# A chunked state-space layer with a mixture of low-rank adapters on one core: who turns x of chunk 1 to tokens in the paired groups

## What is computed

```python
proj = jnp.einsum('bld,pd->blp', hidden_states, in_proj_w)      # gate | x, B, C | dt
xBC = jax.nn.silu(conv)                                          # x: 64 heads of 64; B, C: 8 groups of 128
dt_p = jax.nn.softplus(dt + dt_bias)
dA = jnp.exp(dt_p * A)
dtx = dt_p[..., None] * x
def step(state, inp):
    dA_t, dtx_t, B_t, C_t = inp
    state = state * dA_t[..., None, None] + dtx_t[..., None] * B_t[:, :, None, :]
    y_t = jnp.einsum('bhpn,bhn->bhp', state, C_t)
    return (state, y_t)
y = ys + x * D[None, None, :, None]
yn = (yg * lax.rsqrt(var + EPS)).reshape(B, L, I) * norm_weight
yn = yn * jax.nn.silu(gate)
out = jnp.einsum('bli,di->bld', yn, out_proj_w)
return x + out + base(xn) + lora(xn)
```

## Time and profile before

| | |
|---|---|
| median of 3 runs | 3184.14 us (3183.57 to 3185.0) |
| the profiled execution | 3184.15 us |
| its span, first to last instruction | 3182.3 us |
| granted TensorE clock | 1.00 |
| busy: TensorE, VectorE | 99%, 75% |
| busy: ScalarE, GpSimd | 49%, 27% |

### The profile page before, as it was taken

One profiled execution on the slowest core, in us unless ns is written; L12 is line 12 of the kernel. 1 busy time (PEld: TensorE's weight loads), 2 busy tenths in 40 slices (PEclk: granted clock), 3 DMA queues, 4 the chain that ended last, 5 costly groups with the idle time before them and its releaser, 6 DMA issues.

```text
span 3182.3 us, 55652 instructions
## 1 busy us (share of the span) xinstructions
PE 3164.0 (99%) x17996; PEld 2605.4 (82%) x17996; DVE 2383.3 (75%) x4437; ACT 1548.9 (49%) x3816; POOL 844.9 (27%) x917
## 2 busy tenths in 40 slices
PE   8999999999999999999999999999999999999999
PEld 7788888887888888888788888888878888888887
DVE  7977777786587778777658878787755887787873
ACT  5666656673354444454235545445423544444441
POOL 4444434343022222222102222222210222222220
PEclk9999999999999999999999999999999999999999
DMA  7777777776665555556466555555557655555554
GB/s 287 274 267 263 267 276 263 273 263 247 240 210 181 189 189 187 190 185 207 159 232 201 189 185 189 192 183 193 194 171 234 200 185 186 192 189 196 183 188 159
DMA packets 185673, 672.69 MB, mean 211 GB/s; under 512 B 21056, under 2 KB 22208, under 8 KB 185408
## 3 DMA queue, kind: packets, MB, share of 16 engines
q1 hardware_dynamic: 161280, 584.91, 54.0%
q10 hardware_dynamic: 24128, 84.42, 7.9%
HBM read 532.41 MB, written 136.84 MB: 210 GB/s over the span
## 4 chain that ended last, share of the span: by engine, by line
PE 95%; DVE 3%; DMA 1%; issue 1%; ACT 0%; SPq 0%; POOL 0%; ACTq 0%; DVEq 0%; POOLq 0%
PE dense L1038 27%; PE dense L1040 27%; PE dense L1039 27%; PE pY L1136 3%; PE pD L1166 2%; PE pD L1136 1%; DVE conv_us L1448 1%; PE dense L1075 1%; PE pU L1038 1%; PE pCB L1113 1%; PE pS L1040 1%; PE pS L1038 1%; PE pS L1039 1%; PE pU L1040 1%; PE pU L1039 1%; PE pX L1108 1%
## 5 line engine op out<-in xcount | busy, mean ns | idle before, releaser
L1038 PE MATMUL dense<-xn_hi,w_hl 128*128 128x512 f32 (+1 forms) x2888 | 1143.8, 396 | 1.3 <-ACT conv_us L702 0.9
L1040 PE MATMUL dense<-xn_hi,w_hl 128*128 128x512 f32 (+1 forms) x2888 | 1125.2, 390 | 0.0
L1039 PE MATMUL dense<-xn_lo,w_hl 128*128 128x512 f32 (+1 forms) x2888 | 1123.3, 389 | 0.0
L1040 PEld LDWEIGHTS dense<-xn_hi,w_hl 128*128 128x128 f32 (+1 forms) x2888 | 540.2, 187 | 116.1
L1038 PEld LDWEIGHTS dense<-xn_hi,w_hl 128*128 128x128 f32 (+1 forms) x2888 | 540.7, 187 | 114.4 <-issue 3.0
L1039 PEld LDWEIGHTS dense<-xn_lo,w_hl 128*128 128x128 f32 (+1 forms) x2888 | 541.0, 187 | 111.0 <-issue 1.9
L1448 DVE SCALAR_TENSOR_TENSOR conv_us<-conv_in,const_g,conv_us 128x512 f32<-128x512 f32 x576 | 467.4, 812 | 139.1 <-ACT conv_us L683 124.9
L1038 PE MATMUL dense<-z_hi,w_hl 128*128 128x512 f32 x1024 | 406.2, 397 | 2.0 <-DVE acc L1588 1.5
L1040 PE MATMUL dense<-z_hi,w_hl 128*128 128x512 f32 x1024 | 399.3, 390 | 0.0
L1039 PE MATMUL dense<-z_lo,w_hl 128*128 128x512 f32 x1024 | 398.6, 389 | 0.0
L1588 DVE TENSOR_TENSOR acc<-acc,dense 128x512 f32<-128x512 f32 x256 | 175.2, 685 | 208.1 <-PE dense L1040 198.3
(11 more groups left out here) (202 smaller groups left out, 4447.2 us busy)
## 6 DMA issues: line engine op xcount, KB each, us to landing
w_hl<-w_split SPq DMA_DIRECT2D x732, 512.0 KB, 3.5
w_split<-w_hl SPq DMA_DIRECT2D x244, 512.0 KB, 3.6
cum_b<-cum_scratch ACTq DMA_DIRECT2D x128, 512.0 KB, 4.9
w_raw<-w_slots_dram SPq DMA_DIRECT2D x122, 512.0 KB, 5.1
acc<-x_tr_dram ACTq DMA_DIRECT2D x16, 512.0 KB, 6.3
out_tr_dram<-acc ACTq DMA_DIRECT2D x16, 512.0 KB, 4.8
BC<-x_tok_dram SPq DMA_DIRECT2D x6, 512.0 KB, 5.1
conv_us<-x_tok_dram SPq DMA_DIRECT2D x6, 512.0 KB, 5.8
```

The lines of the kernel that those rows point to most:

```text
L1038: nc.tensor.matmul(out, lhs[0], rhs[0], start=start, stop=False)
L1039: nc.tensor.matmul(out, lhs[0], rhs[1], start=False, stop=False)
L1040: return nc.tensor.matmul(out, lhs[1], rhs[0], start=False, stop=stop)
```

## The change

Chunk 1 is added to the chunks that VectorE turns in the paired groups:

```diff
-        BY_DVE = (0, 2, 3)
+        BY_DVE = (0, 1, 2, 3)
```

## The result

The changed kernel takes 3189.04 us (median of 20 runs, 3186.04 to 3192.31) against 3183.31 us before (20 runs beside them, 3182.27 to 3185.0): ratio 1.0018, 95% interval 1.0012 to 1.0024. It is slower by 5.7 us, and its runs scatter more than twice as wide. The forecast was 3184.7, within 3178 to 3192, and "no change" within 0.2%: it holds, but the sum in it was +0.5 us where +5.7 came. The profiled execution spans 3187.1 us (3182.3 before), so 4.8 us of the loss stand in it.

A forecast was written before the change was run, and what follows sets the result against it. TensorE was taken to bound the kernel (busy 3164.0 of 3182.3 us). After the hold, +1.8 us in 18 groups and -1.3 in the three groups 7 gave +0.5, so 3184.7 us, range 3178 to 3192 for 8 in 10.

The forecast's parts named there:

- What the removed work is worth: TensorE's four x transposes at chunk 1 of each paired group: 0.44 us, 21 times, 9.2 us in all.
- The first twelve transposes are free: VectorE's eight before chunk 0's first y and four between the first unit's adds fit into idle time.
- The hold: Chunk 1: S_lo holds const_g and dtx, third add late, fifth half unit waits 0.54 us; +1.8 us in 18 groups.
- Groups 7: Three groups without const_g: second matmul at 1504.76 instead of 1505.19, 0.43 us stays won each, 1.3 us in all.
- The groups behind the branch: Six groups behind VectorE's loop branch: first add ends 1318.87, TensorE wants its bank at 1318.90; costed at nothing, no slack.
- a wait at the half units ahead of the fifth: Sign named in advance that the prediction is wrong: TensorE waiting at half units before the fifth.
- What is late next: VectorE's lag of about 1.7 us at the third add is worked off in idle time before fourth and sixth adds.
- The transposes are simply won: Rival: nothing held in chunk 1, third add ends 1233.36, all 9.2 us stay, 3174.9 us; chance 0.15.
- Two reads are held: Rival: wx and xD both meet GpSimd, second matmul 0.44 us later in 18 groups, 3191.8 us; chance 0.10.
- The third: Rival: change hits another wait, behind the branch or later in the chain, a few us either way; chance 0.05.
- the 6.4 that were called "same": A measurement of this kernel tells about 0.2% (6.4 us) from no change; "same" had chance 0.72.
- the likeliest case: Break-even within some 0.15 us a group, one instruction held by S_lo; chance 0.70, own range 3181 to 3188.

The follow-up runs named there:

- TensorE's half alone: Kernel before with TensorE's four x transposes of chunk 1 in paired groups left out and nothing in their place (wrong x): 3173.6 us.
- both causes away: Changed kernel with VectorE's loop over pairs written out and the high halves of C and the state made behind chunk 1's exps: 3173.68 us.
- the kernel before with the edits: Kernel before, chunk 1 turned by TensorE, with loop written out, late high halves and third add first: 3182.38 us.
- The run with S_lo late: Changed kernel with ScalarE's high halves of C and the state made behind chunk 1's exps, so GpSimd's S_lo comes later: 3183.07 us.
- the three other versions with the added transposes and the branch: Changed kernel with S_lo late, 3183.07 us; with the third add moved up, 3185.73; with chunk 1's x still read from PSUM, 3188.36.
- the two written-out kernels: VectorE's loop over pairs written out, no branch inside a block: changed kernel 3183.68 us, kernel before 3183.15 us.
- the run with the third add moved up: Changed kernel with the loop written out and the third add ahead of masked CB, B_lo and x times D: 3178.37 us.
- VectorE's lost 4.6 alone: Changed kernel making the 16 added transposes unused, chunk 1's x still transposed by TensorE and read from PSUM: 3188.36 us.
- the changed kernel without the branch: Changed kernel with VectorE's loop over pairs of groups written out: 3183.68 us, ratio 1.0001.

## Why the prediction was right or wrong

**What the removed work is worth** (0.44 us, 21 times): right; 10.1 us in TensorE's half alone, 9.2 with both causes away (8.7 against the kernel before with the edits), beside 9.2.

**The first twelve transposes are free:** right in the 12 ordinary groups, where the first two adds still wait for TensorE. In the three groups 7 they no longer wait, but nothing is lost by it; in the six behind the branch it was wrong.

**The hold:** right in kind and size. dtx was forecast 2.99 behind the second add's start and stands 2.98 behind it; the add's end 5.88, measured 5.85; the loss against before 0.10, measured 0.07 in the matmul's place and 0.08 to 0.14 in the distance to the next group, where that group is not behind a branch. The run with S_lo late takes only its neighbour away and leaves VectorE's program alone, and the wait goes.

**Groups 7:** right. In blocks 1 and 2 dtx was held by S_lo (0.80 us) and the second matmul comes 6.49 behind chunk 1's start instead of 6.92, so 0.43 us stays won; in block 3 it is 6.60.

**The groups behind the branch:** this is the step that failed, "I cost that at nothing, but there is no slack left". By the prediction's own sign, a wait at the half units ahead of the fifth, it was wrong: three of the six groups have one (0.20 to 0.28 us). It went wrong in two ways.

First, the reckoning stopped at the first add. The prediction's row has that add at 1318.18, so 0.40 ahead of chunk 1 (1318.58); the second add follows 1.97 us later by the changed kernel's rows, which makes it 1.3 us later than in an ordinary group. There the held const_g delays dtx from 2.39 to 3.27 behind chunk 1's start (S_lo late, and changed kernel), so the hold hides a lateness of up to 0.9 us and all beyond it reaches the third add. By this working, an estimate from rows of both kernels, done for each of the six with its rows of before, about 0.9 us were to be added in all if the branch took as long as in the profile before.

Second, and this is most of it, the branch took longer than before. VectorE's idle issue ahead of its transposes, all of it in these six groups, is 20.9 us in the changed kernel's profile and 16.3 before. For group 3 of block 1 it is 3.35 instead of 2.76, and the same working then gives 0.8 us; the second matmul is 0.78 later than in an ordinary group. The prediction had the price ("each microsecond by which that branch got longer would cost 6 us in all"), but took the length of before. Whether the added work makes the branch longer isn't settled: with VectorE's program unchanged (TensorE's half alone) it is 18.6 us, in the three other versions with the added transposes and the branch 18.9 to 21.4, and only versions with them show a second idle time, always in block 3.

In the profile the six groups lose 0.90, 0.32, 0.54, 0.78, 0.96 and 0.95 us against the distances before, 4.5 us together, and 0.9 more stand ahead of the two of block 3, where TensorE waits for conv_us. The rest of the 12 ordinary groups' distances lose about 1.0, the groups 7 win 1.2, and all ahead of block 1's group 1 is 0.4 shorter: 4.8 us, as in the spans. The forecast of +0.5 is close to what the two written-out kernels differ by.

**What is late next:** the lag at the third add was as forecast (1.65 us), but it isn't worked off before the fourth and the sixth add. VectorE idled 0.87 and 0.30 us there, less than 1.7; in the changed kernel it doesn't idle at either, and the seventh add still ends 0.33 us later than before, at 20.36 behind chunk 1's start. It costs nothing here, and did in the run with the third add moved up.

**The rivals.** "The transposes are simply won" did not come, and would have with the hold and the branch out of the way. "Two reads are held" did not come in chunk 1. The third, given 0.05, was the one that made the difference.

**The chances:** a change of +5.7 us is on the near side of the 6.4 that were called "same"; the interval of the ratio is clear of 1. The time lies 1.0 above 3181 to 3188, the likeliest case's own range. That the wider range held it is luck: its upper end was set by a rival, two held reads, that is not what cost the time.

## What to carry to other kernels

Before work is moved onto an engine with slack, look for the group, not the average, in which that engine is latest: here six of 21 groups behind a loop's branch decided. Follow its lateness through every later release that the bounding engine wants, not only the first, and don't take an idle time of one execution for a constant where no slack is left. Where operands move from PSUM to SBUF along with the work, write down which GpSimd instruction runs beside each new two-SBUF read; moving that one instruction, by way of the ScalarE copy ahead of it, was worth more than moving VectorE's add (3173.7 against 3178.4, the loop written out in both). And when a change is nearly neutral, measure its halves: here TensorE's half won 10.1 us alone, VectorE's lost 4.6 alone, and together they lost 5.7, so the halves don't add up (-10.1 and +4.6 would be -5.5).

## What the runs showed of the hardware that was not expected

The idle time at the branch is not a constant. In the kernel before it is 2.34 to 3.39 us in the six places of one execution; in the changed one it is 2.76 to 3.58, with 1.18 and 1.15 more a moment later in two of them; in the run with S_lo late 2.27 to 3.55. The profile puts it on no engine ("issue"). What VectorE does in it was not shown; that the branch is its place is, since the written-out loop has none of the six waits.

Stream transposes are not held by GpSimd: 150 of the changed kernel's run wholly while GpSimd works on S_dec, C_lo, S_lo or wx_lo, and none takes over 0.308 us.

That const_g is held was forecast from one row of before. The runs show how it grows: 34 columns, one SBUF operand read and one written, take 0.17 us alone, 1.06 when started 1.02 us before S_lo's end, and 1.15 when started 1.11 before it (block 3 of the changed kernel without the branch). Being short does not help it; whatever stands behind it waits too.
